# Two transformer layers in one kernel: where small loads, first tiles, projection banks and a norm's scale are placed

## The chip, the cores and the metric

The kernel runs on one core of a Trainium2 chip. The metric is the time of one execution on the device in microseconds (us); lower is better. A core has a matmul engine (TensorE; PE in the profile, PEld for its weight loads), VectorE (DVE), ScalarE (ACT), GpSimd (POOL) and SyncE (SP), which here only starts transfers. The engines run side by side, each through its own list of instructions in order, and wait for each other on semaphores.

## What is computed

Two batches of 1024 rows of 512 numbers, float32. Layer 1 is attention with 16 heads of 128 in a band of blocks, with a residual and a norm. Layer 2 picks 128 rows of each batch by a router's score and runs a full layer on those 256 rows only; the others pass unchanged, and everything is normed again. Since the second norm's input is x + x for a row that was not picked, and x is itself normed, its mean is nearly zero.

```python
x = layernorm(x + attention1(x, Wq, Wk, Wv, Wo))      # softmax over |block_i - block_j| <= 2, blocks of 64
scores = x @ w_router                                 # layer 2
idx = sort(top_k(scores, 128))                        # per batch
s = x[idx]
h = rms_norm(s, ln1_w)
q, k, v = h @ wq + bq, h @ wk + bk, h @ wv + bv       # rotated by position, causal over the 256 rows
x1 = s + attention2(q, k, v) @ wo
h2 = rms_norm(x1, ln2_w)
processed = x1 + silu(h2 @ w_gate) * (h2 @ w_up) @ w_down
gate = sigmoid(scores[idx])
out2 = x with rows idx set to gate * processed + (1 - gate) * s
x = layernorm(x + out2)
```

## The kernel before

**Numbers.** Matmuls of layer 1 and of the last stage work on pairs: ScalarE writes a rounded part ("hi", L1155), VectorE or GpSimd the rest ("lo", L1356 and L1664), and three products of the parts are summed (L885). Layer 2's projections and attention take plain float32 (L893).

**Order.** The program first writes one list of jobs, `order`, and every engine then walks the same list and emits its share. So the list fixes each engine's order, and a job placed early or late is so on all engines. `hold` and `freed` say who has to be done before a tile or a bank is written again. The main loop runs over u = 0 to END + 3 with END = 256: head H = u // 8 (0 to 31, two batches of 16), row tile i = u % 8. One step has three score matmuls, half a projection of q or k (`project_qk`), the transposes of the last tile's probabilities, the product with v, and, by its place in a group of two heads (16 steps), one tile of v (`project_v`) or of the output projection (`project_out`). On VectorE a step begins with the row maximum of the scores (L1391), and after ScalarE's exponential (L1193) come the scaling (L1400) and the lo parts. At the end of a step at most one piece of weights is split; two are when two are due.

**Start.** L724 to 739: eight tiles of x are loaded, four ahead of the first three weights and four behind; eight transposes (L912) into the eight banks, then the first projections of q and k, both into "proj0".

**Norms.** `finish_layer1` (L496) norms a tile of layer 1: statistics on VectorE (L1455, L1456), reciprocal root and shift on GpSimd (L1637, L1639, L1678), the row on ScalarE (L1239), the router's score on VectorE (L1465). `finish_plain` (L513) does the same for the second norm of rows that pass: job "pl", with four operations on GpSimd, and "plnorm" on ScalarE (L1246). For batch 0 this runs in steps 132 to 150, while batch 1's tiles are transposed in; for batch 1 the plain norms run in the last stage.

**Layer 2.** `choose` finds the rows and gathers them. `routed_in` has the gated rows' score and squares ("rin": L1522, L1525 on VectorE, an exponential on ScalarE L1261, L1637 and L1639 on GpSimd), the product with the norm's weights (L1533, followed by three small operations, L1537 to L1539) and four transposes (L1046), copied to hT ("rinh"). In step END - 4 = 252 stand, in this order: eight loads of layer 2's weights (`load_home`), the clearing of a tile for the biases (L1424), their load (L1772), that of the norm's weights (L1767), the split of the biases on ScalarE and VectorE, "rin" of batch 0; "rinh" follows in step 253. `project2` computes the projections of layer 2 in eight parts per batch, alternately in "proj0" and "proj1"; their bank is free when VectorE has rotated them (L1552 to L1556; v: when ScalarE has copied it). The rotated sum (L1557) is transposed (L1072). VectorE may rotate only when layer 1's last product with v is done, since the targets lie where layer 1's tiles are. The last stage is gate, up and down (`gate_up`, `down`).

## Time and profile before

| | us |
|---|---|
| median of 3 runs (1348.3 to 1349.73) | 1348.95 |
| the profiled execution | 1349.21 |
| its span, first to last instruction | 1347.5 |
| mean granted clock of the matmul engine | 0.985 |

| engine | share of the span | instructions |
|---|---|---|
| matmul engine | 95% | 7296 |
| VectorE | 59% | 2219 |
| ScalarE | 45% | 1422 |
| GpSimd | 18% | 234 |

The busy shares are means over stages that differ: in the steps of layer 1 the matmul engine has work all the time, in the change from layer 1 to layer 2 VectorE has. A time line row says when an instruction (or a run of equal ones, "x4") starts, how long it takes, the engine, the line of the kernel that emits it, and in brackets how long the engine had stood idle and who released it. Lines 885, 893, 1155, 1356 and 1664 are helpers, so a row is known by its tiles: "proj" is a projection bank, "s" scores, "o" products with v, "y" the output projection, "arena" the pairs, "wraw" raw weights, "late" layer 2's tiles, "works" working tiles. The clock is the granted one: 1.00 is 2.4 GHz, 0.50 is 1.2 GHz.

### The profile page before, as it was taken

Reading aid. Unit: us, or ns where it says so; the run is one execution under the profiler, and the core shown is the slowest. Engines: PE = TensorE matmul, PEld = TensorE weight load, DVE = VectorE, ACT = ScalarE, POOL = GpSimd, SP = SyncE. Lnnn points to the kernel's source line nnn. Section 1 sums busy time; section 2 is a strip of 40 time slices with the busy share of each in tenths; the row PEclk is TensorE's granted clock in tenths of the full one; section 3 lists DMA queues with packets and bytes.
Section 4 is the critical chain, followed back from the end, with each engine's and each line's share of the span. In section 5 each row is a group of like instructions: output and inputs, shape, how many; then the busy total and the mean of one; then the engine's idle time right before and its main releaser. Section 6 shows DMA issues by size and latency. Waiting matters only on the chain.

```text
span 1347.5 us, 19014 instructions
## 1 busy us (share of the span) xinstructions
PE 1280.1 (95%) x7296; PEld 1092.8 (81%) x7296; DVE 793.1 (59%) x2219; ACT 605.1 (45%) x1422; POOL 247.8 (18%) x234
## 2 busy tenths in 40 slices
PE   6999999999999999999999999999999858999897
PEld 5998989898989898977798989898989744445696
DVE  4656665666566656676767765666566557542244
ACT  4544445444444445445444444444544333434353
POOL 2111111111111101133121121111111121000186
PEclk9999999999999999999999999999999979999898
DMA  5110100110101202033210101010101225564064
GB/s 166 46 32 24 40 32 32 32 32 32 32 32 36 75 1 78 1 102 104 93 48 17 48 28 48 29 34 32 32 32 32 95 98 185 180 205 156 0 196 133
DMA packets 62411, 89.34 MB, mean 66 GB/s; under 512 B 3232, under 2 KB 36000, under 8 KB 62320
## 3 DMA queue, kind: packets, MB, share of 16 engines
q1 hardware_dynamic: 61904, 86.81, 19.8%
q0 software_dynamic: 416, 1.31, 0.3%
q8 instruction: 57, 0.93, 0.3%
q14 instruction: 34, 0.28, 0.1%
HBM read 79.20 MB, written 8.91 MB: 65 GB/s over the span
## 4 chain that ended last, share of the span: by engine, by line
PE 83%; DVE 8%; ACT 4%; POOL 2%; DMA 2%; issue 1%; SPq 0%; ACTq 0%; POOLq 0%; DVEq 0%
PE proj L885 38%; PE y L885 12%; PE o L885 9%; PE s L885 9%; PE tp L964 5%; PE proj L893 4%; PE s L893 3%; DVE arena L1356 2%; ACT arena L1155 2%; PE o L893 1%; POOL arena L1664 1%; DMA wraw<-in_L_ffn_w_up 1%; DVE prob L1391 1%; ACT prob L1193 1%; DVE products L1465 1%
## 5 line engine op out<-in xcount | busy, mean ns | idle before, releaser
L885 PE MATMUL proj<-arena 128*128 128x256 f32 (+1 forms) x3456 | 636.2, 333 | 6.8 <-DVE arena L1356 6.6
L885 PEld LDWEIGHTS proj<-arena 128*128 128x128 f32 x3456 | 529.2, 190 | 67.4 <-DVE arena L1356 10.6
L1193 ACT ACTIVATE prob<-prob,stat 128x384 f32<-128x384 f32 (+1 forms) x256 | 151.0, 590 | 445.0 <-DVE stat L1391 445.0
L1664 POOL TENSOR_TENSOR arena<-wraw,arena 128x1024 fp32r<-128x1024 f32 x75 | 181.8, 2432 | 841.3 <-ACT arena L1155 841.3
L1356 DVE TENSOR_TENSOR arena<-proj,arena 128x512 fp32r<-128x512 f32 (+1 forms) x262 | 146.5, 560 | 279.6 <-ACT arena L1155 278.2
L885 PE MATMUL y<-arena 128*128 128x512 f32 x762 | 198.6, 396 | 0.5 <-DVE yacc L1441 0.5
L885 PE MATMUL o<-arena 128*128 128x256 f32 (+2 forms) x960 | 196.4, 324 | 0.4 <-DVE arena L1356 0.2
L1356 DVE TENSOR_TENSOR arena<-tp,arena 128x384 fp32r<-128x384 f32 (+2 forms) x257 | 133.9, 521 | 103.9 <-ACT arena L1155 103.6
L885 PE MATMUL s<-arena 128*128 128x384 f32 (+2 forms) x870 | 191.1, 332 | 3.3 <-DVE arena L1356 3.2
L1155 ACT ACTIVATE arena<-proj 128x512 fp32r<-128x512 f32 (+1 forms) x262 | 127.6, 488 | 120.7 <-PE proj L885 114.8
L885 PEld LDWEIGHTS s<-arena 128*128 128x128 f32 x870 | 151.5, 188 | 20.8 <-DVE arena L1356 4.5
L885 PEld LDWEIGHTS y<-arena 128*128 128x128 f32 x762 | 138.6, 189 | 23.6 <-DVE yacc L1441 1.0
L885 PEld LDWEIGHTS o<-arena 128*128 128x128 f32 x960 | 136.8, 191 | 1.6 <-DVE arena L1356 1.1
L1391 DVE CUSTOM_DVE_ANT_0 prob<-s,band 128x384 f32<-128x384 f32 (+1 forms) x256 | 131.7, 515 | 0.7 <-PE s L885 0.7
L964 PE MATMUL tp<-ident,prob 128*128 128x128 f32 x704 | 119.8, 274 | 4.3 <-DVE prob L1400 4.3
L1155 ACT ACTIVATE arena<-tp 128x384 fp32r<-128x384 f32 (+2 forms) x257 | 117.4, 457 | 8.0 <-PE tp L964 7.9
L1400 DVE TENSOR_SCALAR prob<-prob,stat 128x384 f32<-128x384 f32 (+1 forms) x256 | 111.3, 435 | 9.1
L964 PEld LDWEIGHTS tp<-ident,prob 128*128 128x128 f32 x704 | 86.3, 140 | 21.1 <-DVE prob L1400 10.1
L1441 DVE TENSOR_TENSOR yacc<-y,yacc 128x512 f32<-128x512 f32 x127 | 87.1, 686 | 18.9 <-PE y L885 18.8
L1155 ACT ACTIVATE arena<-wraw 128x1024 fp32r<-128x1024 f32 x88 | 90.7, 1055 | 6.7 <-DMA wraw<-in_L_ffn_w_up 4.1
L893 PE MATMUL proj<-late 128*128 128x512 f32 x128 | 61.8, 606 | 4.0 <-DVE late L1556 4.0
L1155 ACT ACTIVATE arena<-o 128x512 fp32r<-128x512 f32 (+2 forms) x73 | 41.4, 567 | 27.1 <-PE o L1046 15.0
(153 smaller groups left out, 700.5 us busy)
## 6 DMA issues: line engine op xcount, KB each, us to landing
wraw<-in_L_attn_Wq SPq DMA_DIRECT2D x16, 512.0 KB, 3.4
wraw<-in_L_attn_Wk SPq DMA_DIRECT2D x16, 512.0 KB, 3.3
wraw<-in_L_attn_Wv SPq DMA_DIRECT2D x16, 512.0 KB, 3.3
wraw<-in_L_attn_Wo SPq DMA_DIRECT2D x16, 512.0 KB, 3.6
late<-in_L_ffn_wq SPq DMA_DIRECT2D x16, 512.0 KB, 4.7
late<-in_L_ffn_wo SPq DMA_DIRECT2D x16, 512.0 KB, 3.9
yacc<-in_L_attn_hidden_states SPq DMA_DIRECT2D x16, 256.0 KB, 3.0
y_dram<-yacc SPq DMA_DIRECT2D x16, 256.0 KB, 3.0
```

The costliest lines, as they stand in the source:

```text
L885: ins = e.matmul(out_ap, l[a], r[b], start=first and i == 0 and j == 0, stop=final and i == n - 1 and j == 2, skip_group_check=skip)
L893: ins = e.matmul(out_ap, l, r, start=first and i == 0, stop=final and i == n - 1, skip_group_check=skip)
L964: ins = e.transpose(bank["tp"][:, m * P:(m + 1) * P], prob[i % 2][:, m * P:(m + 1) * P], ident[:])
L1155: e.activation(dst, src, ACT.Copy).then_inc(*S_.inc(*name, "hi"))
L1193: e.activation(prob[s][:, 0:n], prob[s][:, 0:n], ACT.Exp, bias=stat[:, 4 * s + 1:4 * s + 2], scale=-1.0, accum_out=stat[:, 4 * s + 2:4 * s ...
L1356: e.tensor_tensor(dst_lo, src, dst_hi.bitcast(F32), ALU.subtract).then_inc(*V_.inc(*name, "lo"))
L1391: e.tensor_tensor_reduce(prob[s][:, 0:n], bank[f"s{s}"][:, 0:n], reach, -SCALE, -NEG, ALU.add, ALU.min, nm).then_inc(*V_.inc("scores", H, ...
L1400: e.tensor_scalar(prob[s][:, 0:n], prob[s][:, 0:n], rc, None, ALU.mult).then_inc(*V_.inc("norm", H, i, "prob"))
L1441: e.tensor_tensor(yacc[:, t, :], bank[bank_of["out", G, t]][:, :], yacc[:, t, :], ALU.add).then_inc(*V_.inc("out", G, t, "sum"))
L1465: e.tensor_tensor_reduce(products[:], row, router[:], 1.0, 0.0, ALU.mult, ALU.add, score[:, c:c + 1]).then_inc(*V_.inc("lnscore", b, t, "s ...
L1664: e.tensor_tensor(lo, wraw[n % RAW_SLOTS][:], hi.bitcast(F32), ALU.subtract).then_inc(*G_.inc("wsplit", n, "lo"))
```

## The change

- The biases' clearing and load (now job "ubraw") and the load of layer 2's first norm weights go from step 252 to step EARLY = 192. "rin" of batch 0 goes to step 250, its product ("rinx", split off from "rinh") to 251, the transposes and copy to 252, the biases' split to 253.
- At the start two weights are loaded behind x tiles 0 to 3, then tiles 4 to 7, then the third. Tiles 0 to 3 are transposed, then comes the first projection of q, tiles 4 and 5, that of k (in "proj1"), tiles 6 and 7.
- In the first group the projections of q go to bank "y", which the output projection doesn't use there; v's first part in layer 2, the third projection of batch 0, goes to "s1".
- The second norm's scale comes from the first's: with variance v and r = 1/sqrt(v + eps), the second scale on the normed row is 1/sqrt(v r r + eps/4). Three more operations on GpSimd in "ln" write it to eight columns of `stat`; job "pl" is gone; "plnorm" is a copy with that scale, without a shift.
- There are two tiles hT, one per batch.

The diff, cut (renamings and the same edit at further places are left out):

```diff
@@ placements of tiles
-        hT = whole(slot2, KT, P)
+        hT = [whole(slot2, KT, P), whole(slot0 + 2 * HD, KT, P)]
+        twice = stat[:, 8:8 + TT]
@@ project_qk: the bank is a parameter
-        def project_qk(H, which, c):
+        def project_qk(H, which, c, to="proj0"):
...
-            hold("proj0", ("qk", H, which, c), V_, "qk", H, which, c, "lo")
+            bank_of["qk", H, which, c] = to
+            hold(to, ("qk", H, which, c), V_, "qk", H, which, c, "lo")
@@ finish_layer1, finish_plain
+            hold(f"share{t % 2}", ("ln", b, t), G_, "ln", b, t, "twice")
             job("ln", b, t)
...
         def finish_plain(b, t):
-            hold(f"moments{t % 2}", ("pl", b, t), S_, "plnorm", b, t, "row")
-            job("pl", b, t)
             yield
@@ routed_in: jobs of batch 0 taken out, the product a job of its own
-            hold("work5", ("rin", b), T_, "rinh", b, "made")
-            hold("products", ("rin", b), V_, "rin", b, "score")
-            job("rin", b)
             if b == NB - 1:
+                hold("work5", ("rin", b), T_, "rinh", b, "made")
+                hold("products", ("rin", b), V_, "rin", b, "score")
+                job("rin", b)
                 for _ in range(RIN_STEPS):
                     yield "choose"
-            yield "choose"
+                yield "choose"
+            if b > 0:
+                job("rinx", b)
@@ project2
-            to = f"proj{n % 2}"
+            to = "s1" if (b, n) == (0, 2) else f"proj{n % 2}"
@@ start
         for t in range(4):
             load_resid(0, t)
-        load_next()
+        load_next(2)
         for t in range(4, TT):
             load_resid(0, t)
+        load_next()
         job("router")
-        for t, to in enumerate(("proj0", "proj1", "s0", "s1", "o0", "o1", "y", "tp")):
+        for t, to in enumerate(("tp", "s0", "s1", "o0")):
             turn_x(0, t, to)
-            if t == 3:
-                need("q", 0, 0)
-            if t == 5:
-                need("k", 0, 0)
+        need("q", 0, 0)
+        need("k", 0, 0)
         put(project_qk(0, "q", 0))
+        turn_x(0, 4, "o1")
+        turn_x(0, 5, "y")
+        put(project_qk(0, "k", 0, "proj1"))
+        turn_x(0, 6, "tp")
+        turn_x(0, 7, "o0")
         lo_engine[0] = lambda n: "G"
         need("v", 0, 0)
-        put(project_qk(0, "k", 0))
@@ steps: own is the bank of the q projections
+            own = "y" if G == 0 else "proj0"
...
-                    qk_gen = project_qk(H, "q", 1)
+                    qk_gen = project_qk(H, "q", 1, own)
...
-            if u == END - 4:
+            if u == EARLY:
                 hold("work1", ("ubias",), V_, "ubias", "lo")
                 bias_loaded.plan(0)
                 bias_loaded.plan(LO_ROW)
+                job("ubraw")
+                load_ln("work0", 0, V_, "rinx", NB - 1, "h")
+            if u == END - 6:
+                hold("work5", ("rin", 0), T_, "rinh", 0, "made")
+                hold("products", ("rin", 0), V_, "rin", 0, "score")
+                job("rin", 0)
+            if u == END - 5:
+                job("rinx", 0)
+            if u == END - 4:
+                put(routed_in(0))
+            if u == END - 3:
                 job("ubias")
-                load_ln("work0", 0, V_, "rinh", NB - 1, "h")
-                begin(routed_in(0))
@@ ScalarE: ubias, plnorm, rinh
-                    act.wait_ge(*V_.at("ubias", "zero"))
...
-                    act.wait_ge(*G_.at("pl", b, t, "shift"))
-                    e.activation(work[2 + i], yacc[:, t, :], ACT.Identity, bias=shift[i][:], scale=rstd[i][:]
+                    act.wait_ge(*S_.at("lnorm", b, t, "row"))
+                    act.wait_ge(*G_.at("ln", b, t, "twice"))
+                    e.activation(work[2 + i], yacc[:, t, :], ACT.Copy, scale=twice[:, t:t + 1]
...
-                    act.wait_ge(*T_.at("out", NB * NG - 2, TT - 1, "made"))
-                    if b > 0:
-                        act.wait_ge(*T_.at("p2", b - 1, len(QKV_ORDER) - 1, "made"))
+                    act.wait_ge(*T_.at("out", NB * NG - 2 + b, TT - 1, "made"))
@@ VectorE: ubraw is the clearing, ln alone takes statistics
+                elif kind == "ubraw":
+                    dve.wait_ge(*freed("work1", "ubias"))
+                    e.memset(work[1][0:BIAS_ROWS, :], 0.0).then_inc(*V_.inc("ubraw", "zero"))
...
-                elif kind in ("ln", "pl"):
+                elif kind == "ln":
@@ GpSimd: ln
+                    e.tensor_scalar(tmp[i][:], mv[i][:, 1:2], rstd[i][:], rstd[i][:], ALU.mult, ALU.mult
+                                    ).then_inc(*G_.inc("ln", b, t, "share"))
+                    pool.wait_ge(*G_.at("ln", b, t, "share"))
+                    e.tensor_scalar(tmp[i][:], tmp[i][:], 0.25 * LN_EPS, None, ALU.add).then_inc(*G_.inc("ln", b, t, "more"))
+                    pool.wait_ge(*G_.at("ln", b, t, "more"))
+                    if b > 0:
+                        pool.wait_ge(*S_.at("plnorm", b - 1, t, "row"))
+                    e.tensor_tensor(twice[:, t:t + 1], tmp[i][:], neg_half[:], ALU.pow).then_inc(*G_.inc("ln", b, t, "twice"))
@@ SyncE: the biases' loads hang on the new job
-                elif kind == "ubias":
-                    sp.wait_ge(*V_.at("ubias", "zero"))
+                elif kind == "ubraw":
+                    sp.wait_ge(*V_.at("ubraw", "zero"))
```

## Rows read from the trace of the kernel before

**Rows 1.** Page, part 1: busy time, share, instructions by engine.

```profile
PE 1280.1 (95%) x7296; PEld 1092.8 (81%) x7296; DVE 793.1 (59%) x2219; ACT 605.1 (45%) x1422; POOL 247.8 (18%) x234
```

**Rows 2.** Waits of the matmul engine: waiter <- releaser, us, times, longest.

```profile
PE proj L885 <- DVE arena L1356: 6.6, 9, 1.5
```

**Rows 3.** Stretches: length, busy time by engine, granted clock, DMA share, GB/s.

```profile
572.00:653.00 81.00, 73.38 (x408) 60.79 (x406) 58.61 (x160) 40.47 (x90) 28.37 (x58) 1.00 0.30 98
...
1089.70:1120.50 30.80, 28.75 (x115) 20.30 (x115) 19.21 (x62) 10.12 (x22) 8.45 (x19) 0.92 0.33 108
...
1275.00:1332.00 57.00, 57.00 (x413) 54.05 (x412) 27.90 (x35) 32.42 (x51) 43.29 (x46) 1.00 0.55 171
```

**Rows 4.** Time line, VectorE, 631.7 to 632.6: start, us, engine, instruction.

```profile
631.72 0.66 DVE L1455 BATCH_NORM_STATS2 bn_out<-yacc 128x6 f32<-128x512 f32 x1
...
632.51 0.39 DVE L1356 TENSOR_TENSOR arena<-proj,arena 128x256 fp32r<-128x256 f32 x1
```

**Rows 5.** Time line, all engines, 1066 to 1096.5 us.

```profile
1066.79 1.06 ACT L1155 ACTIVATE arena<-wraw 128x1024 fp32r<-128x1024 f32 x1
...
1068.05 0.68 DVE L1441 TENSOR_TENSOR yacc<-y,yacc 128x512 f32<-128x512 f32 x1
...
1069.01 0.60 ACT L1155 ACTIVATE arena<-proj 128x512 fp32r<-128x512 f32 x1 [1.16 <-PE proj L885]
...
1073.56 0.55 DVE L1391 CUSTOM_DVE_ANT_0 prob<-s,band 128x384 f32<-128x384 f32 x1
...
1076.60 0.48 DVE L1424 MEMSET works<- 40x512 f32 x1
...
1083.23 0.63 ACT L1155 ACTIVATE arena<-works 40x512 fp32r<-40x512 f32 x1 [7.83 <-DMA works<-bqkv]
...
1084.60 0.69 DVE L1522 CUSTOM_DVE_ANT_0 products<-x_sel,router 128x512 bf16<-128x512 f32 x1
...
1085.44 1.99 ACT L1155 ACTIVATE arena<-wraw 128x1024 fp32r<-128x1024 f32 x2
...
1086.83 5.11 POOL L1664 TENSOR_TENSOR arena<-wraw,arena 128x1024 fp32r<-128x1024 f32 x2
...
1086.88 2.84 DVE L1533 SCALAR_TENSOR_TENSOR works<-x_sel,gate,works 128x512 f32<-128x512 f32 x1 [0.49 <-POOL gate L1639]
...
1089.78 1.12 PE L1046 MATMUL proj<-ident,works 128*128 128x128 f32 x4 [15.08 <-DVE gate L1537]
...
1095.79 0.55 DVE L1391 CUSTOM_DVE_ANT_0 prob<-s,band 128x384 f32<-128x384 f32 x1
```

**Rows 6.** Instructions of line 1533, two executions: shortest, median, longest in ns.

```profile
L1533 DVE SCALAR_TENSOR_TENSOR works<-x_sel,gate,works x2: 731/1785/2839, 1086.9 to 1179.5; 128x512 f32<-128x512 f32 x2
```

**Rows 7.** Time line, all engines, the first 30 us.

```profile
9.86 1.22 DVE L1356 TENSOR_TENSOR arena<-wraw,arena 128x1024 fp32r<-128x1024 f32 x1 [0.26 <-ACT arena L1155]
...
12.21 1.97 PE L912 MATMUL o<-ident,yacc 128*128 128x128 f32 x8 [3.96 <-DMA yacc<-in_L_attn_hidden_states]
...
20.30 2.98 PE L885 MATMUL proj<-arena 128*128 128x512 f32 x12 [1.50 <-DVE arena L1356]
...
20.53 2.40 POOL L1664 TENSOR_TENSOR arena<-wraw,arena 128x1024 fp32r<-128x1024 f32 x1 [17.39 <-ACT arena L1155]
...
24.70 0.63 PE L885 MATMUL s<-arena 128*128 128x256 f32 x3 [1.41 <-DVE arena L1356]
...
27.95 0.69 PE L885 MATMUL s<-arena 128*128 128x384 f32 x3
```

**Rows 8.** Time lines of VectorE and the matmul engine, 1124 to 1130 us.

```profile
1124.63 0.69 DVE L1557 TENSOR_TENSOR late<-late 128x512 f32<-128x512 f32 x1
...
1126.74 0.69 DVE L1557 TENSOR_TENSOR late<-late 128x512 f32<-128x512 f32 x1
...
1124.65 3.07 PE L893 MATMUL proj<-late 128*128 128x512 f32 x4 [4.03 <-DVE late L1556]
...
1129.76 1.88 PE L893 MATMUL proj<-late 128*128 128x512 f32 x4
```

## What the change will do to the time

> **What bounds the kernel now.** I read the page first: the matmul engine is busy for 1280.1 of 1347.5 us [rows 1], so a gain can only come from the 67 us in which it stands still or runs slowly. The list of waits of that engine then gives the places: one wait of 15.08 us at the first transposes of layer 2, and nine waits on the low parts of layer 1 that sum to 6.6 [rows 2, 5]. The table of stretches shows a third sum: from 572 to 653 us, where batch 0 is normed and batch 1 is brought in, the engine works 73.38 of 81.00 us, 7.6 less than it could [rows 3]. The time lines of these places [rows 5, 7, 8] show what is late in each. In the last stage (1275 to 1332) the engine is busy 57.00 of 57.00 us [rows 3]: what is taken from other engines there is worth nothing. The profiled execution took 1349.21 us (span 1347.5 and 1.7 around it), the median is 1348.95; I work against 1349.2.
>
> **The small loads long ahead (steps 250 to 254): gain 10.2.** Now, in step 252, VectorE clears a tile, SyncE sends the biases behind eight weight loads, and ScalarE stands 7.83 us until they land; the gated rows' scores, squares and product stand behind that on VectorE, the transposes (L1046) behind them on the matmul engine [rows 5]. The change issues both loads 60 steps earlier (cost: a clearing of 0.48 us [rows 5], beside matmuls), and spreads the rest over steps 250 to 253. The 15.08 us don't all come back, because the steps from 251 on are short and run at VectorE's chain, not at the matmuls. I follow the row maximum of each tile on VectorE. Before, that of step 252 starts at 1073.56, that of 254 at 1095.79 [rows 5]. After:
> - Step 250 gets the gated rows' score and squares (2 x 0.69, [rows 5]) and ScalarE an exponential between them and its own work. The score can start when the sum at 1068.05 is over, 1068.7, and ends at 1069.4. Until then ScalarE may do neither the weight split that it now does at 1066.79 (1.06 us) nor the projection part that it now does at 1069.01 [rows 5]. So 1069.4 + 0.2 + 1.06 = 1070.7 for a part that ran at 1069.01: +1.7 on the chain.
> - Step 251 gets the product and three small operations. Alone the product takes 0.73, beside a split on GpSimd 2.84 [rows 6]. In this step GpSimd is likely through its one split; I take 0.73 and about 0.4 for the small ones: +1.1.
> - So the maximum of step 252 stands at 1073.56 + 2.8 = 1076.4. A tile takes 3.04 us on this chain (1073.56 to 1076.60, [rows 5]); two make 6.1. Into them go the first output sum (0.6), the bias parts (ScalarE 0.63, about as much on VectorE: 1.3), and two weight splits that now fill the standstill: 1.99 us on ScalarE, 5.11 on GpSimd [rows 5]. Of ScalarE's 1.99 I put 1.2 on the chain. That is 1076.4 + 6.1 + 0.6 + 1.3 + 1.2 = 1085.6 for 1095.79: 10.2.
> The gain holds the half clock too: the granted clock is 0.92 from 1089.7 to 1120.5 [rows 3], that is 5 of the 30.8 us at 1.2 GHz, behind the standstill. Bounds: without the +1.7 and 1.2, and with 0.5 less for the biases, 13.6; with VectorE held by the splits for 3.4 more, 6.8. The order on the matmul engine has the transposes one step earlier; its ready product comes before them, so they cost their own 0.65.
>
> First the row: the product starts at 1086.88, 0.05 us behind GpSimd's split, and takes 2.84 instead of 0.73 [rows 5, 6]. The Trainium skill (SBUF — State Buffer, section "SBUF: two separate sides") says that VectorE in a two-port mode or with two SBUF inputs and GpSimd lock a shared port for a whole instruction, and the other fully blocks. The trace agrees. By that rule the scalings of steps 253 and 254 could each be held for one split; it speaks against a full gain, and is the second rival below.
>
> **Start: gain 2.7.** Now the x tiles 4 to 7 come behind three weights, and the projections behind all eight transposes: tile 4 is turned at 12.21 and the first projection waits behind tile 7, although its weights' low part is ready at 9.86 + 1.22 = 11.08 [rows 7]. After: the query projection at 11.1 (its 12 matmuls take 2.98 by the second one's row, [rows 7]) to 14.1, two tiles of 0.85 each (half of 8 transposes in 1.97, less overlap) to 15.8, the key projection to 18.7 (in the second bank: no 1.50 us wait [rows 7]), two tiles to 20.4. First scores 24.70 to 20.4. But the value weights now land behind the x tiles and ScalarE splits them behind tile 7: about 22.2, so GpSimd's low part comes 22.3 to 24.7, where it now ends at 22.9 [rows 7]. The first value matmuls start at 24.8, the second scores at about 26.1 instead of 27.95: 1.85 stay. The third bank ("y", free in the first group) takes away two more waits of 0.4 each among the nine: 0.8. Sum 2.7; bounds 1.0 (value weights 1.7 later) and 5.1 (the whole 4.3).
>
> **One norm's scale from the other's (572 to 653): gain 4.5.** Per tile VectorE loses statistics and aggregate, 0.80 us from 631.72 to 632.51 [rows 4]; eight tiles make 6.4. ScalarE's plain norm stays in its place, but doesn't wait for GpSimd. The chain of this stretch lies mostly on VectorE and ScalarE; I take 0.56 of each 0.80, since ScalarE is next late: 4.5. Bounds: 1.0, where other waits take its place, and 7.6, where no standstill is left [rows 3]. GpSimd does three operations (some 1 us) more per norm and four fewer per plain norm; the additions stand behind the shift, so nothing of the same tile waits for them. Where two norms follow each other without a gap (tiles 6 and 7 of batch 1), the second shift comes 1 us later; its row of scores is needed over 10 us later. Batch 1's removed statistics lie in the saturated last stage: 0.
>
> **Third projection bank and two hT: gain 1.1.** The third projection of layer 2 starts at 1124.65 after a wait of 4.03 us for the rotation of the first, which frees its bank [rows 8]. In "s1" it runs in the wait, 1120.6 to 1122.2. The turning of the first needs VectorE's sum, which starts at 1124.63, that of the second the one at 1126.74 [rows 8]: the matmul engine reaches the third's second half at 1127.9 and not at 1129.76: 1.86. But it still stands most of 1122.2 to 1127.4, and its matmuls there run at half clock (3.07 us for four, [rows 8]); I keep 1.1, bounds 0.4 and 1.9. The second hT frees batch 1's copy from batch 0's last projection, which is long over by then: 0.
>
> **Sum.** 10.2 + 2.7 + 4.5 + 1.1 = 18.5: 1349.2 - 18.5 = 1330.7.
>
> **Rivals.**
> - The waits vanish more fully (0.17): ScalarE's part of the gate finds a gap, and VectorE had slack. 13.6 + 4.3 + 6.4 + 1.9 = 26.2: 1323.0. For it: the removed wait was of 15.08 and the clock came back late. Against: the 3.04 us pitch is already VectorE's.
> - GpSimd's splits block VectorE in the short steps, and ScalarE holds tiles and splits together (0.25): 6.8 + 2.0 + 3.0 + 0.4 = 12.2: 1337.0. For it: 2.84 against 0.73 [rows 6]. Against: the product slipped in between two splits.
> - It does not do what it says (0.07): the transposes stay late, because rows gathered, statistics and reciprocal root on GpSimd are behind a split, not the loads. Then only about 2 of the 10.2 come: 1338.9.
> - Slower (0.03): many standstills of 1 to 3 us from step 251 to 256 hold the clock at 1.2 GHz until about 1120. From 1089.7 to 1120.5 there are 28.75 us of matmul work [rows 3]; at half clock it takes as much again, 2.5 of which is paid now, and 2.3 for the 2.3 us of step 252 and 253 come on top. It decides from 21 us on: the whole gives 28.5 - 18.5 = 10 over, 1359. Against it: steps as thin as these ran within the stretch whose mean clock is 0.92 [rows 3].
> - The parts cancel to within 2.7 us (0.03): 1348.
> The forecast has 0.45, its own range 1326 to 1335. The range of 8 in 10 takes in most of the first two rivals: 1322 to 1339. A measurement can tell 0.2% (2.7 us) from no change: faster 0.94, same 0.03, slower 0.03.
>
> **What would show it.** The wait at L1046 for layer 2's first transposes under 2 us; the first scores near 20.4 and the second near 26.1; the maximum of step 254 about 10 us nearer to that of step 252; 572 to 653 shorter by 4.5; no wait above 3.5 us behind the last layer-1 output. Wrong if ScalarE stands behind the gate's exponential for more than 3 us, if the stretch of the norms keeps its length, or if a half clock appears between steps 250 and 256.

## The result

| | before | after |
|---|---|---|
| median (range), us | 1348.63 (1348.3 to 1349.73) | 1332.78 (1330.49 to 1335.49) |
| the profiled execution, us | 1349.21 | 1332.4 |
| its span, us | 1347.5 | 1330.3 |
| mean granted clock | 0.985 | 0.986 |

The ratio is 0.9882 (95% interval 0.9862 to 0.9902), 15.9 us; by the spans it is 17.2. The forecast was a gain of 18.5 us and a time of 1330.7. Part 1 of the page of after, which answers to [rows 1]:

```profile
PE 1279.7 (96%) x7296; PEld 1092.9 (82%) x7296; DVE 781.6 (59%) x2187; ACT 602.9 (45%) x1422; POOL 243.3 (18%) x218
```

The matmul engine has the same instructions and the same busy time to 0.4 us, so all of the gain is time in which it no longer stands. Its list of waits in after (waiter <- releaser, us, times, longest):

```profile
PE y L1097 <- DVE late L1582: 8.9, 6, 3.1
PE tp L989 <- DVE prob L1423: 7.1, 7, 1.9
PE proj L909 <- DVE arena L1379: 6.3, 8, 2.9
...
PE y L1097 <- ACT late L1184: 1.7, 1, 1.7
...
PE proj L1071 <- DVE gate L1562: 0.2, 1, 0.2
```

The wait of 15.08 us at layer 2's first transposes [rows 5] is 0.2 (last line). The low parts of layer 1 cost 6.3 where they cost 6.6 [rows 2], but 2.9 of them is one wait at the first projection, new by design. The longest entry is now layer 2's rotation, 8.9.

**Where the time went.** I took points that both traces have and subtracted their starts. A negative number in the last column is time that the stretch takes more than before.

| point | before | after | us sooner | added by this stretch |
|---|---|---|---|---|
| second scores of the start | 27.95 | 25.48 | 2.5 | 2.5 |
| weight split on GpSimd ahead of the norms | 536.08 | 533.06 | 3.0 | 0.5 |
| weight split behind the norms | 647.38 | 640.23 | 7.15 | 4.1 |
| row maximum of step 252 | 1073.56 | 1068.87 | 4.7 | -2.5 |
| row maximum of step 254 | 1095.79 | 1078.75 | 17.0 | 12.35 |
| last output products of layer 1 | 1118.89 | 1101.86 | 17.0 | 0.0 |
| first scores of layer 2 | 1134.03 | 1119.94 | 14.1 | -2.9 |
| last stage begins | 1267.39 | 1251.17 | 16.2 | 2.1 |
| end of the span | 1347.5 | 1330.3 | 17.2 | 1.0 |

*The start*, time line of the matmul engine in after (start, us, engine, instruction, idle before and its releaser), which answers to [rows 7]:

```profile
10.56 4.61 PE L909 MATMUL proj<-arena 128*128 128x512 f32 x12 [2.89 <-DVE arena L1379]
15.00 0.60 PE L936 MATMUL o<-ident,yacc 128*128 128x128 f32 x4
...
15.79 3.02 PE L909 MATMUL proj<-arena 128*128 128x512 f32 x12
...
20.32 0.59 PE L909 MATMUL s<-arena 128*128 128x256 f32 x3 [0.63 <-DVE arena L1379]
...
23.95 1.69 PE L909 MATMUL proj<-arena 128*128 128x256 f32 x12 [0.86 <-POOL arena L1690]
25.48 0.69 PE L909 MATMUL s<-arena 128*128 128x384 f32 x3
```

The first scores start at 20.32 (forecast 20.4), the second at 25.48 (26.1). But the first projection takes 4.61 us for the 12 matmuls that the second does in 3.02: the clock is half there, behind a standstill of 2.89. That the first scores still come where I put them is luck: the projection starts 0.5 us sooner than I counted, and tiles 4 and 5 take 0.4 us each (15.00 to 15.79) where I had 0.85, and so do tiles 6 and 7.

*The norms*, the stretch of after that answers to [rows 3] (length, busy time of PE, PEld, DVE, ACT, POOL, granted clock, DMA share, GB/s):

```profile
569.50:645.70 76.20, 71.85 (x406) 60.71 (x404) 53.23 (x143) 39.65 (x90) 27.88 (x52) 1.00 0.32 104
```

Nearly the same matmuls (406 for 408) lie in 76.20 us and not in 81.00; of the 7.6 us in which the engine stood, 4.35 are left (76.20 - 71.85). VectorE has 5.4 us less of work. The two windows don't begin and end at quite the same work; between the weight splits of the table, which do, the stretch is 4.1 us shorter.

*Steps 250 to 254*, time line of all engines in after, which answers to [rows 5], and one stretch of it:

```profile
1067.76 0.74 DVE L1558 SCALAR_TENSOR_TENSOR works<-x_sel,gate,works 128x512 f32<-128x512 f32 x1
...
1068.56 0.99 PE L1071 MATMUL proj<-ident,works 128*128 128x128 f32 x4 [0.19 <-DVE gate L1562]
...
1068.87 0.55 DVE L1414 CUSTOM_DVE_ANT_0 prob<-s,band 128x384 f32<-128x384 f32 x1
...
1071.08 2.01 ACT L1180 ACTIVATE arena<-wraw 128x1024 fp32r<-128x1024 f32 x2
...
1072.22 4.70 POOL L1690 TENSOR_TENSOR arena<-wraw,arena 128x1024 fp32r<-128x1024 f32 x2 [6.19 <-ACT arena L1180]
...
1074.57 0.15 DVE L1422 RECIPROCAL stat<-stat 128x1 f32<-128x1 f32 x1
1074.76 2.38 DVE L1423 TENSOR_SCALAR prob<-prob,stat 128x384 f32<-128x384 f32 x1
...
1078.75 0.56 DVE L1414 CUSTOM_DVE_ANT_0 prob<-s,band 128x384 f32<-128x384 f32 x1
```

```profile
1069.00:1075.00 6.00, 4.79 (x16) 3.98 (x15) 3.01 (x11) 5.27 (x12) 2.78 (x2) 0.50 1.00 377
```

The product takes 0.74 for 2.84 and the transposes run one step earlier. From the maximum of step 252 to that of step 254 it is 9.88 us, before it was 22.23. Two of the 9.88 are in one row: the scaling of step 253 takes 2.38 us while GpSimd splits; the usual length of this instruction is 0.42, as below.

The second fence shows that steps 252 and 253 run at half clock: 6.8 us of it, from 1068.7 to 1075.6. Before, there were 17.1 us of half clock at this place (1077.6 to 1094.7), most of it over the standstill. In after it costs nothing that can be seen: the matmul engine is busy for only 4.79 of these 6.00 us and waits for VectorE, and experiment 9 has the same 9.9 us from maximum to maximum with its half clock almost wholly behind them (1077.9 to 1081.4).

*Between the layers*, time line of the matmul engine in after, which answers to [rows 8], and two stretches of it:

```profile
1101.86 1.52 PE L909 MATMUL s<-arena 128*128 128x512 f32 x6
...
1103.43 1.88 PE L917 MATMUL s<-late 128*128 128x512 f32 x4
1108.45 0.63 PE L1097 MATMUL y<-ident,late 128*128 128x128 f32 x4 [3.14 <-DVE late L1582]
1110.76 1.11 PE L1097 MATMUL y<-ident,late 128*128 128x128 f32 x4 [1.69 <-ACT late L1184]
1111.67 3.62 PE L917 MATMUL s<-late 128*128 128x512 f32 x4
...
1115.94 3.78 PE L917 MATMUL proj<-late 128*128 128x512 f32 x4
...
1119.94 0.61 PE L917 MATMUL s<-late 128*128 128x128 f32 x4
```

```profile
1104.00:1109.00 5.00, 1.86 (x8) 0.66 (x6) 4.86 (x13) 0.83 (x2) 2.84 (x8) 1.00 0.80 277
1109.00:1120.00 11.00, 9.31 (x17) 4.09 (x17) 6.25 (x25) 2.49 (x4) 2.16 (x5) 0.53 0.25 85
```

The third projection's first half starts 1.57 us behind the last output products, without a wait, as planned; then the engine stands for 3.14 and 1.69 us, and from 1109.7 to 1120 (10.2 us) the granted clock is 0.5, 1.2 GHz, the half clock: four matmuls take 3.62 and 3.78 us instead of 1.88 and 1.98. Before, the same place had these rows (a stretch, and two of the time line):

```profile
1125.00:1129.00 4.00, 3.58 (x8) 1.42 (x6) 3.93 (x12) 1.20 (x2) 0.45 (x1) 0.57 0.08 11
```

```profile
1131.99 1.98 PE L893 MATMUL proj<-late 128*128 128x512 f32 x4
...
1134.03 0.61 PE L893 MATMUL s<-late 128*128 128x128 f32 x4
```

That is 3.4 us at half clock. From the last output products to the first scores ("the stretch between the layers" below) it was 15.14 us, it is 18.08: the part that I forecast at +1.1 stands at -2.9.

*The last stage.* It is 79.13 us long in after and 80.11 before. Its rows for the sum of the gated rows, before and then after, name the reason:

```profile
1337.54 0.75 DVE L1619 SCALAR_TENSOR_TENSOR works<-s,gate,works 128x512 f32<-128x512 f32 x1 [1.78 <-ACT works L1246]
```

```profile
1320.40 0.75 DVE L1645 SCALAR_TENSOR_TENSOR works<-s,gate,works 128x512 f32<-128x512 f32 x1 [3.21 <-PE s L909]
```

Before, the sum waits for the plain norm on ScalarE (L1246), which waits for GpSimd's shift; in after it waits for the last matmuls. The five profiles without the norm part all have the first wait (1.78 to 1.80) and a last stage of 79.9 to 80.3 us, the nine with it have the second and 78.4 to 79.2. So the norm part is worth another 0.8 to 1.9 us here. The 2.1 us ahead of the last stage are not the change's: 1.7 of them are a half clock at 1244.9 to 1248.3 in before, which eleven of the other twelve profiles have too, with or without the change, and this profile of after lacks.

### The profile page after: what moved, and what is told of

It reads as the page before. It is cut to its first block, busy times and chain, and to the rows that moved or that the text cites. A ratio compares the mean times of both kernels' runs of the same rounds, so it can differ in the third digit from the quotient of the medians.

```text
span 1330.3 us, 18968 instructions
## 1 busy us (share of the span) xinstructions
PE 1279.7 (96%) x7296; PEld 1092.9 (82%) x7296; DVE 781.6 (59%) x2187; ACT 602.9 (45%) x1422; POOL 243.3 (18%) x218
## 4 chain that ended last, share of the span: by engine, by line
PE 87%; DVE 7%; ACT 4%; issue 1%; POOL 1%; DMA 1%; SPq 0%; POOLq 0%
PE proj L909 41%; PE y L909 13%; PE s L909 10%; PE o L909 9%; PE tp L989 5%; PE proj L917 3%; PE s L917 3%; DVE arena L1379 2%; ACT arena L1180 2%; PE o L917 1%; ACT prob L1218 1%; DVE prob L1414 1%; DVE products L1490 1%; DVE prob L1423 1%; DVE yacc L1466 1%
## 5 line engine op out<-in xcount | busy, mean ns | idle before, releaser
L909 PE MATMUL proj<-arena 128*128 128x256 f32 (+1 forms) x3408 | 625.5, 332 | 7.2 <-DVE arena L1379 6.3
L909 PEld LDWEIGHTS proj<-arena 128*128 128x128 f32 x3408 | 521.8, 190 | 65.4 <-DVE arena L1379 8.2
L1379 DVE TENSOR_TENSOR arena<-proj,arena 128x512 fp32r<-128x512 f32 (+1 forms) x256 | 142.7, 558 | 274.2 <-ACT arena L1180 272.4
L909 PE MATMUL y<-arena 128*128 128x512 f32 x810 | 211.0, 396 | 0.3 <-DVE yacc L1466 0.3
L1180 ACT ACTIVATE arena<-proj 128x512 fp32r<-128x512 f32 (+1 forms) x256 | 124.3, 486 | 118.5 <-PE proj L909 115.5
L909 PEld LDWEIGHTS y<-arena 128*128 128x128 f32 x810 | 147.4, 189 | 24.7 <-DVE yacc L1466 0.7
L1466 DVE TENSOR_TENSOR yacc<-y,yacc 128x512 f32<-128x512 f32 x127 | 87.1, 686 | 17.1 <-PE y L909 17.0
L917 PE MATMUL proj<-late 128*128 128x512 f32 x120 | 58.6, 612 | 0.0
L1180 ACT ACTIVATE arena<-o 128x512 fp32r<-128x512 f32 (+1 forms) x74 | 42.0, 568 | 22.6 <-PE o L1071 14.7
```

The source lines that it names most:

```text
L909: ins = e.matmul(out_ap, l[a], r[b], start=first and i == 0 and j == 0, stop=final and i == n - 1 and j == 2, skip_group_check=skip)
L917: ins = e.matmul(out_ap, l, r, start=first and i == 0, stop=final and i == n - 1, skip_group_check=skip)
L1180: e.activation(dst, src, ACT.Copy).then_inc(*S_.inc(*name, "hi"))
L1379: e.tensor_tensor(dst_lo, src, dst_hi.bitcast(F32), ALU.subtract).then_inc(*V_.inc(*name, "lo"))
L1466: e.tensor_tensor(yacc[:, t, :], bank[bank_of["out", G, t]][:, :], yacc[:, t, :], ALU.add).then_inc(*V_.inc("out", G, t, "sum"))
```

## The experiments

Experiments 2, 7 and 8 start from the kernel before, the others from the changed kernel, and their edits are shown against the kernel that they start from (11 and 12 against the one ahead of them). All ratios are to the kernel before, run on the same chip.

**1. The changed kernel without its third bank.**

```diff
-            to = "s1" if (b, n) == (0, 2) else f"proj{n % 2}"
+            to = f"proj{n % 2}"
```

> The changed kernel with the third projection of layer 2 back in the first bank, all else as changed. Theory A, the third bank lengthens the half-clock time: in the changed kernel the matmul engine ran its one projection first and then stood twice (3.14 and 1.69 us) before 1111.7, and the granted clock was half from 1109.7 to 1120.0, where before it was half for 3.4 us. Then without the bank the standstill is one wait of 4 us again, the half clock short, and the median falls by about 3 us below 1332.8, to 1330. Theory B, the half clock there comes with the standstill of VectorE's rotation whatever the bank, and differs from run to run: the median is within 1.5 us of 1332.8 and the profile shows a half clock of some length behind the wait too; by the bank's own 1.1 us the median would be 1333.9.

Measured: 1331.31 us (1329.86 to 1334.51), ratio 0.986 [0.9844, 0.9877]; the whole change is at 0.9882 with an interval that overlaps. Its stretch between the layers is 17.79 us, with the wait that the kernel before had [rows 8] to 0.01 us:

```profile
1102.78 1.52 PE L909 MATMUL s<-arena 128*128 128x512 f32 x6
...
1108.56 3.78 PE L917 MATMUL proj<-late 128*128 128x512 f32 x4 [4.04 <-DVE late L1581]
```

With the same waits as before (4.04 and 0.69) the stretch is 2.65 longer than before. Its half clock is 10.2 us, before it was 3.4. So the long half clock can come without the bank. That the bank has no part in it isn't shown: this is one profile, and by the ratios (0.986 against 0.9882, intervals that overlap) the kernel is, if anything, 3 us faster without the bank. The table behind experiment 12 has all profiles.

**2. The bank alone, in the kernel before** (the same line, the other way round).

> The kernel before with the third projection of layer 2 in the bank s1 and nothing else. The stretch from the last output products to the first scores of layer 2 takes 15.1 us before, with 3.4 us at half clock in it. Theory A (the forecast): the third projection runs inside the wait, 1.1 us gained (0.4 to 1.9). Theory B, by the runs so far: the stretch is set by VectorE's second rotation and ScalarE's copy, and the bank moves matmuls only within it; 0 to 0.5 us at equal clock, and the median within 1 us of before, either way, by the length of the half clock.

Measured: 1350.62 us against 1350.17, ratio 1.0001 [0.9992, 1.001]: the bank is worth nothing, between -1.4 and +1.1 us. The time line of the matmul engine tells why:

```profile
1119.32 1.52 PE L885 MATMUL s<-arena 128*128 128x512 f32 x6
...
1120.89 1.88 PE L893 MATMUL s<-late 128*128 128x512 f32 x4
1125.90 1.08 PE L1072 MATMUL y<-ident,late 128*128 128x128 f32 x4 [3.12 <-DVE late L1557]
1128.01 1.09 PE L1072 MATMUL y<-ident,late 128*128 128x128 f32 x4 [1.03 <-DVE late L1557]
1128.89 3.62 PE L893 MATMUL s<-late 128*128 128x512 f32 x4
...
1135.00 0.61 PE L893 MATMUL s<-late 128*128 128x128 f32 x4
```

The third's second half starts 9.57 us behind the last output products; before it was 1129.76 - 1118.89 = 10.87. That is a gain of 1.3 us, where I counted 1.86 and kept 1.1. But these four matmuls take 3.62 us at half clock, which lasts 6.8 us here and 3.4 before, and the scores come 15.68 behind the products instead of 15.14.

**3. Does a shorter standstill keep the clock?** In the steps of the main loop `tick("p2r")` leaves the rotations out; in the last step (259) the first rotation is now advanced too, and so goes ahead of the last two output sums and their norms on VectorE.

```diff
-            tick("p2r")
+            tick(*(("p2r",) if u < END + 3 else ()))
```

> The changed kernel with the rotation of layer 2's first projection placed in the last step of the main loop (259), before the last two output sums and their norms on VectorE, and not after them. Theory A, the place in VectorE's order makes the 3.14 us wait and the half clock behind it: the rotation, ready some 10 us earlier, goes into VectorE's idle time near 1097 to 1102; the waits at the two transposes before 1111 fall under 1 us each, the half clock there is gone, and the median is 1332.8 - 4.8 (waits) - 3 (half clock) = 1325 to 1328. Theory B, VectorE has no slack there (it is the bound): what the rotation gains the last norms lose, the rows of scores come later, and the median stays within 1.5 us of 1332.8.

Measured: 1329.96 us (1329.54 to 1330.6), ratio 0.9856 [0.9839, 0.9872]. The stretch between the layers is 12.0 us, and its clock is whole (the stretch, then the time line):

```profile
1103.00:1116.00 13.00, 9.85 (x38) 5.40 (x37) 12.62 (x44) 4.50 (x7) 7.54 (x18) 1.00 0.63 198
```

```profile
1103.83 1.52 PE L909 MATMUL s<-arena 128*128 128x512 f32 x6
...
1106.20 0.66 PE L1097 MATMUL y<-ident,late 128*128 128x128 f32 x4 [0.63 <-DVE yacc L1466]
...
1111.09 0.63 PE L1097 MATMUL y<-ident,late 128*128 128x128 f32 x4 [2.51 <-DVE late L1582]
...
1115.83 0.61 PE L917 MATMUL s<-late 128*128 128x128 f32 x4
```

The first transposes wait for an output sum (0.63), which frees their bank, and no longer for the rotation (3.14). The 6.1 us that the stretch lost split into waits that went (3.14 + 1.69 - 0.63 - 2.51 = 1.7) and 4.4 that are nearly all the clock. This is one profiled execution; by the medians the gain is 2.8 and by the ratios 3.5, with intervals that just overlap, so in others the clock is likely low here or elsewhere (in this one the start had 6.8 us of it). The forecast of 1325 to 1328 was missed, and so was its sign that both waits fall under 1 us: the second is 2.51.

**4. The changed kernel once more**, beside the kernels of 8 to 10.

> The changed kernel itself, on the chip of the next three. By the runs so far its times spread from 1330.5 to 1335.5 where the kernel before spreads over 2 us. Theory: the spread is the length of the half clock in the thin stretches; this profile then shows the stretch from the last output products to the first scores of layer 2 between 16 and 18 us, by a half clock of 6.8 or 10.2 us, and a median of 1331 to 1335.

Measured: 1335.77 us (1332.7 to 1337.18), ratio 0.9884 [0.9869, 0.99]: the ratio holds (0.9882). The waits of the first and second transposes are 3.14 and 1.68, the stretch between the layers 18.09, the half clock 10.2 again.

**5. The norm part undone.** Statistics, job "pl" and the old "plnorm" are back.

```diff
-                elif kind == "ln":
+                elif kind in ("ln", "pl"):
...
-                    e.activation(work[2 + i], yacc[:, t, :], ACT.Copy, scale=twice[:, t:t + 1]
+                    e.activation(work[2 + i], yacc[:, t, :], ACT.Identity, bias=shift[i][:], scale=rstd[i][:]
```

> The changed kernel with the plain norm as before: its own statistics on VectorE and its own root on GpSimd, no scale from the first norm. Theory A, the removed statistics were on VectorE's chain where batch 0 is normed: the stretch between the two weight splits at 533 and 640 us is 4.1 us longer again and the median is 1332.8 + 4.1 = 1337. Theory B, the 4.1 us came from the third operand, the wait of ScalarE's plain norm for GpSimd, with the same sum. Theory C, the extra operations on GpSimd cost in the change between the layers (the second shift late by 1.3 us, ScalarE's copy behind it): then 4.1 - 1.3 = 2.8, 1335.6.

Measured: 1339.36 us (1337.51 to 1340.41), ratio 0.9926 [0.991, 0.9943]. From the weight split ahead of the norms (533.53) to the one behind them it is 111.33 us; in the kernel before 111.30, in after 107.17:

```profile
644.86 2.39 POOL L1689 TENSOR_TENSOR arena<-wraw,arena 128x1024 fp32r<-128x1024 f32 x1 [3.24 <-ACT arena L1181]
```

So the part is worth 4.2 us in its stretch. By the ratios it is 0.9926 - 0.9882 = 0.0044 or 5.9 us, and by the spans 5.5. More than the stretch is behind that: the wait for the plain norm at the end is back (1.79), and the last stage is 79.93 us long, 0.8 and 1.5 more than in the two profiles of the changed kernel.

**6. The bank "y" undone** (`own = "proj0"`).

> The changed kernel with all projections of q in the first group in the first bank again. Theory A (the forecast): bank y takes away two waits of 0.4 us, so the median is 1332.8 + 0.8 = 1333.6, and waits of projections on the low parts between 26 and 80 us are back. Theory B: nothing to measure, within 0.5 us, since the next wait takes their place.

Measured: 1333.89 us, ratio 0.9886 [0.9869, 0.9903], not to be told from the whole change. Between 24 and 80 us it has a wait of 0.42 at a projection and one of 0.28 at scores, where the changed kernel has one of 0.61 at scores. From the second scores to the same transposes near 81 us it is 56.05 us, in after 55.57: the bank is worth half a microsecond, less than a median shows.

**7. The new start alone** (with bank "y"), in the kernel before.

```diff
-        load_next()
+        load_next(2)
         for t in range(4, TT):
             load_resid(0, t)
+        load_next()
...
         put(project_qk(0, "q", 0))
+        turn_x(0, 4, "o1")
+        turn_x(0, 5, "y")
+        put(project_qk(0, "k", 0, "proj1"))
...
```

> The kernel before with the new start alone (two weights before tiles 4 to 7, projections between the transposes, q's projections of the first group in bank y). Theory A: 3.0 us, as the weight split at 536 us comes 3.0 sooner in the changed kernel; second scores at 25.5 instead of 27.95. Theory B: the start gains less where the clock is half over the first projection (3.4 to 6.8 us in four of the profiles): 1.5 to 3 by the run.

Measured: 1347.21 us against 1350.17, ratio 0.998 [0.997, 0.9989], that is 2.7 us (1.5 to 4.1). The weight split ahead of the norms comes at 533.33 instead of 536.08, 2.75 sooner. The first projection is slow here as well:

```profile
10.83 4.61 PE L890 MATMUL proj<-arena 128*128 128x512 f32 x12 [2.89 <-DVE arena L1362]
```

**8. The loads and the gated rows alone**, in the kernel before.

```diff
+            if u == EARLY:
...
+                job("ubraw")
+                load_ln("work0", 0, V_, "rinx", NB - 1, "h")
+            if u == END - 6:
...
+                job("rin", 0)
+            if u == END - 5:
+                job("rinx", 0)
...
```

> The kernel before with the small loads alone moved to step 192 and the gated rows' work to steps 250 to 253: no other part of the change. Theory A (the forecast): 9.8 to 10.2 us, 1348.6 - 10 = 1338.6, with the wait at the first transposes of layer 2 under 0.5 us, and the maximum of step 254 about 12.5 us behind that of step 252 instead of 22.2. Theory B, the part is worth its wait (15.1 and the half clock behind it): 1332. Theory C, it depends on the shorter norms before it: under 8.

Measured: 1340.39 us (1339.34 to 1341.97), ratio 0.9924 [0.9909, 0.994], 10.3 us. The maxima of the steps show both signs of the forecast:

```profile
1075.82 0.55 DVE L1405 CUSTOM_DVE_ANT_0 prob<-s,band 128x384 f32<-128x384 f32 x1
...
1085.71 0.56 DVE L1405 CUSTOM_DVE_ANT_0 prob<-s,band 128x384 f32<-128x384 f32 x1
```

Step 252 comes 2.3 us later than before, step 254 10.1 sooner (forecast: 2.8 later, and 1085.6 for 1085.71). The last output products start at 1108.91, 9.98 sooner; 0.28 of that is there at the weight split ahead of the norms (535.80 for 536.08), before the part begins, which leaves 9.7. The stretch between the layers is 15.34, with a half clock of 3.4 us.

**9. The gated rows long ahead.** "rin" and "rinx" of batch 0 in steps 216 and 217.

```diff
-            if u == END - 6:
+            if u == END - 40:
...
-            if u == END - 5:
+            if u == END - 39:
```

> The changed kernel with the gated rows' score, squares and product of batch 0 in steps 216 and 217 and no more in 250 and 251. Theory A (the sum of the prediction): in step 250 ScalarE stands for the exponential and does the weight split before the projection's part, and step 251 has the product; together they moved the row maximum of step 252 by 2.5 us. Early, these cost nothing beside the matmuls; the maximum of step 252 comes 2.5 us sooner and the median is 2 to 2.5 us below the changed kernel's. Theory B, GpSimd's splits block the scaling of step 253 wherever the rest stands (it took 2.38 for 0.42): then they take up part of it, and 0.5 to 1 us is left.

Measured: 1330.79 us, ratio 0.9848 [0.9833, 0.9863]. From the maximum of step 248 (1051.36) to that of step 252 (1068.20) it is 16.84 us, in the changed kernel on the same chip 19.33 (1050.75 to 1070.08): 2.49. This is the price of the gated rows in steps 250 and 251. It isn't all won: in their new place they cost 0.7, since from the weight split behind the norms to the maximum of step 248 it is 410.00 us here and 409.27 in the changed kernel (409.9 to 410.0 in all four profiles with the gated rows this early, 409.2 to 409.4 in the ten others). So the move nets 1.8. The medians differ by 5.0 (1335.77 to 1330.79) and the spans by 2.9; in the profiles 2.0 of that is a shorter half clock between the layers (6.8 us for 10.2). From step 252 to 254 it stays at 9.89, so the gated rows have no part in these.

**10. Both, 3 and 9.**

> The last one and the rotation of layer 2's first projection in step 259, together. Apart they gave 3.5 by the ratios (rotation) and, by the sum, 2.3. If they are independent the median is 1332.8 - 3.5 - 2.3 = 1327; if the rotation's gain is only the phase of the half clock, it is gone here in part: 1329 to 1330.

Measured: 1328.47 us (1327.69 to 1330.82), ratio 0.9832 [0.9818, 0.9845], between the two forecasts (1327; 1329 to 1330), and with an interval that overlaps that of experiment 9. The clock came back less well than in 3: the stretch between the layers is 15.11 and has a half clock of 6.8 us,

```profile
1110.00:1117.00 7.00, 7.00 (x11) 2.58 (x10) 3.90 (x20) 1.89 (x3) 2.43 (x5) 0.54 0.38 130
```

though the order of work there is that of experiment 3, with the same two waits (0.63 and 2.51), and there the half clock is missing.

**11. No weight splits in steps 252 to 254.** Added to 10; it tests whether GpSimd's splits hold VectorE.

```diff
-            else:
+            elif u < END - 4:
                 split_loaded(was_loaded)
```

> The kernel with both early parts, and without the two weight splits in steps 252 to 254 (they come behind the choice of rows). Theory A, they are what is left on the chain: in step 253 the scaling took 2.38 us for 0.42 beside GpSimd's split, and ScalarE's 2 us of splits held the exponential for 0.6; without them the maximum of step 254 comes 2.5 us sooner behind that of 252 (9.9 to 7.4) and the median falls from 1328.5 to 1326. Theory B, the output product's place on the matmul engine sets these steps: under 1 us.

Measured: 1324.68 us (1323.99 to 1326.69), ratio 0.9814 [0.9801, 0.9827]. VectorE in the kernel of 10, then in this one:

```profile
1073.43 2.39 DVE L1423 TENSOR_SCALAR prob<-prob,stat 128x384 f32<-128x384 f32 x1
```

```profile
1073.82 0.42 DVE L1423 TENSOR_SCALAR prob<-prob,stat 128x384 f32<-128x384 f32 x1
```

Without a split beside it the scaling takes 0.42 us, and steps 252 to 254 take 7.30 for 9.89: 1.97 from the scaling, the remaining 0.6 from the parts on ScalarE (two weights there take 2.01 us in one piece, behind which the exponential of step 253 comes 1.20 us behind its maximum and not 0.59). By the ratios the whole gain is 2.4 us.

**12. The best of these, with two more steps.** The value weights' low part at the start on VectorE, and the second rotation advanced ahead of the last stage.

```diff
-        lo_engine[0] = lambda n: "G"
         need("v", 0, 0)
+        lo_engine[0] = lambda n: "G"
...
+        tick(only="p2r")
         lo_engine[0] = lambda n: "V"
```

> The last one, with the second rotation of layer 2 placed before the last two norms on VectorE, and the low part of the first value weights on VectorE and not GpSimd. The second transposes of layer 2 lose their wait of 2.5 us, the first value products one of 0.9; sum against the last one 2.5 + 0.9 = 3.4 where no half clock stands in the stretch, so 1322.6. Rival: the rows of scores of tiles 6 and 7, 2.1 us later on VectorE, become the bound of the choice of rows: 1325.

Measured: 1325.05 us (1322.24 to 1325.34), ratio 0.981 [0.9797, 0.9823]. It is faster than the kernel before and the changed kernel, but isn't to be told from experiment 11; the forecast was 1322.6, and its rival gave 1325. The wait for the value weights (0.86) is gone, and the first two scores follow each other in 4.03 us instead of 5.18. The second transposes wait about as long as before (2.63 for 2.51), but they come sooner:

```profile
1103.05 0.63 PE L1098 MATMUL y<-ident,late 128*128 128x128 f32 x4 [2.63 <-DVE late L1583]
1103.51 5.30 PE L918 MATMUL s<-late 128*128 128x512 f32 x8
```

They start 5.66 us behind the last output products (1097.39), in experiment 11 it was 7.25. VectorE does take the second rotation 1.6 us sooner. But in experiment 11 the first half of the third projection (1.88 us) ran inside that wait; here it comes behind the transposes and makes a run of eight with the second half. So the first scores of layer 2 come 13.81 us behind the products, in experiment 11 13.56, and the gain is gone.

**All profiles, between the layers.** The time from the last output products to the first scores of layer 2, and the half clock in it:

| kernel | third bank | first rotation | half clock | stretch |
|---|---|---|---|---|
| before, 7, 8 | no | late | 3.4, 3.4, 3.4 | 15.14, 15.19, 15.34 |
| 1 | no | late | 10.2 | 17.79 |
| 2 | yes | late | 6.8 | 15.68 |
| 5, 6, 9 | yes | late | 6.8, 6.8, 6.8 | 15.94, 16.16, 16.12 |
| after, 4 | yes | late | 10.2, 10.2 | 18.08, 18.09 |
| 3, 10, 11, 12 | yes | early | 0, 6.8, 3.4, 3.4 | 12.00, 15.11, 13.56, 13.81 |

With the bank and the late rotation no profile has less than 6.8 us; without the bank three of four have 3.4. That speaks for a part of the bank in the long half clock, and experiment 1 against it; with one profile a kernel it stays open. The early rotation makes the stretch shorter in all four than it is in any with the bank and the late rotation.

## Why the prediction was right, and where it wasn't

The time came out 2.1 us above the forecast, within the forecast's own range; the gain was 15.9 us by the ratio, 2.6 short of 18.5. Two of the four terms have their measured size, that of the norm is right for its place and lacks another one, and the fourth isn't there. That the sum comes so close is in part luck, as the last part of this section says.

**Loads, forecast 10.2: right.** Alone they gave 9.7 us in the trace and 10.3 by the ratio; in the whole change 12.35 - 2.5 = 9.85. The inner steps hold too. Step 252 is late by 2.5 (forecast 2.8), and experiment 9 shows that it is the gated rows: 2.49. Steps 252 to 254 were put at 6.1 + 0.6 + 1.3 + 1.2 = 9.2; measured 9.88. The last term was sized by the wrong engine: I booked 1.2 us for two splits on ScalarE; experiment 11 gives 2.6 for all the splits, 1.97 of it as one blocked scaling on VectorE. That is the second rival's mechanism, seen once: two splits in a row on GpSimd take 4.70 us, and VectorE was held for most of the second. The scaling of step 254 took 0.42.

The other terms of the 9.2 were put at 8.0 together and are 7.30 in experiment 11, so two errors offset each other by half. The pitch of 3.04 us that I took for a tile is the distance from a maximum to a clearing, not to the next maximum; the maxima of steps 252 and 253 are 2.9 apart.

A scaling with one input in 32-bit numbers was held for 1.97 us, where the product that I cited has two inputs. The Trainium skill (SBUF — State Buffer, section "SBUF: two separate sides") names both kinds, an instruction in a two-port mode and one with two SBUF inputs, as holders of the shared port. By that rule the scaling is of the first kind; the trace agrees that it can be held (2.38 us for 0.42), and doesn't show its mode. The page says of GpSimd and VectorE alike that the one that is first blocks the other for the whole instruction; here the scaling started at 1074.76, near the start of the second split by an even division of the row (1072.22 + 4.70 / 2 = 1074.57), and ended at 1077.14, just behind that split's end at 1076.92. That fits; the row doesn't show where one split ends and the next begins.

**Start, forecast 2.7: right in sum.** Alone it gave 2.7 by the ratio and 2.75 in the trace. Errors inside it offset each other. The second scores are 2.5 sooner and not 1.85, because the value weights' low part was ready at 23.95 and not at 24.8. The query projection came at 10.56 and not 11.1, but took 4.61 us at half clock, where I took 2.98 from a row at full clock; the tiles behind it took 0.4 us each and not 0.85; and the bank "y" gave about 0.5 instead of 0.8.

**Norm, forecast 4.5: right in its stretch, and a term is missing.** 4.1 between the splits, and 4.2 when undone. The 0.56 of 0.80 us a tile was a choice; measured is 4.2 / 8 = 0.52. The step that failed is "Batch 1's removed statistics lie in the saturated last stage: 0". The stage is saturated only until the last matmuls; at its end VectorE stood 1.78 us for the last plain norm, and without that wait the stage is 0.8 to 1.9 us shorter over the profiles. Undone, the whole part costs 5.5 by the spans and 5.9 by the ratios.

**Third bank, forecast 1.1: wrong.** The step that failed is "the matmul engine reaches the third's second half at 1127.9 and not at 1129.76 ... I keep 1.1". Reaching it sooner is true: 9.81 us behind the last output products in after, 9.57 with the bank alone, 10.87 before. It was to be 1.86 and is 1.1 and 1.3. That it stays until the scores is false: from there to the first scores it was 4.27 before and is 8.27 in after (6.11 with the bank alone). I had read a half clock in the rows and treated it as a fixed property of the place, of a known length; its length is what changed, 3.4 before, 6.8 with the bank alone, 10.2 in both profiles of the changed kernel and in the one without the bank. Isolated, the bank gains 0.0 us (between -1.4 and +1.1). The -2.9 of the table of points is the clock's: the two waits sum to 4.83 us in after and 4.72 before, and the other 2.8 are matmuls that take longer. With the bank alone the waits are 0.57 shorter (4.15) and the matmuls 1.11 longer.

**The sum.** The parts by themselves give 10.3 + 2.7 + 5.5 + 0.0 = 18.5 us (the third by the spans of experiment 5), each known to 1 or 2 us, and the whole gives 15.9. What is lost on the way has the size of the 2.9 us between the layers, which none of the parts run alone has; that it is this loss isn't shown. The 17.2 of the spans is flattered: -2.9 between the layers stands there against +2.1 up to the last stage, of which 1.7 is a half clock that the profile of before has at 1244.9 to 1248.3 and that of after happens to lack. Against the forecast, an error of -4.0 between the layers is met there by 1.0 at the end of the last stage and by 2.1 that isn't the change's: that the spans come within 1.3 us of 18.5 is in part luck. The other runs of after reach from 1330.5 to 1337.2 where those of before mostly stay within 4 us: that fits half clocks of different length in one place, but I have a trace of only one execution of each series.

**Rivals.** "More fully" fell: ScalarE's part of the gate found no gap (2.5 lost). "GpSimd blocks" was true in kind, at 2.0 us where I had put 3.4. "Doesn't do what it says" fell with the wait at the transposes, 0.2. "Slower by half clock" put the half clock between steps 251 and 256. It was there, for 6.8 us over steps 252 and 253, and it was one of the prediction's signs of being wrong. But it cost nothing, since the matmul engine isn't the last there; the sign was badly chosen. The half clock that cost came behind the layer, 10.2 us at a price of about 4.4. Of the other signs, the first scores, the wait at the transposes and the waits behind the layer (3.31 at most) came out as said. "About 10 us nearer" for the maxima of steps 252 and 254 was 12.35; by the prediction's own working it should have read 13.0.

**What stays open.** Why the half clock lasts 3.4, 6.8 or 10.2 us. Experiments 3 and 10 have the same order of work in that place and the same waits, and one has none and the other 6.8. Whether the third bank makes it longer is open too, by the table behind experiment 12. No run here settles either.

## What to carry over

- A wait of 15 us on a bound engine is worth what the next chain leaves: follow the engine that will be last (here the row maximum on VectorE) step by step through the place. This gave 10.2 for a wait of 15.08, and 9.7 to 10.3 was measured.
- Work that is moved out of a full spot should go well beyond it. Six steps ahead the gated rows still cost 2.5 us, forty steps ahead 0.7; and the wait that was left was refilled by weight splits that cost 2.6.
- A stage that is saturated on average has an end where it is not. What is taken from the other engines is worth nothing up to the last matmul and can count behind it.
- Where the matmul engine is thin between two phases, count what you gain there at the end of the thin place, not inside it: the clock can take it back. Shortening the standstill itself (experiment 3, 3.5 by the ratios) gave more than keeping the engine busy around it (the bank, 0.0).

## What the runs showed of the hardware that I had not expected

- The granted clock falls to 0.5 also at the start, behind a standstill of 2.89 us that follows the transposes of the first four tiles: 12 matmuls in 4.61 us for 3.02. All eleven profiles with this start have them slow (4.44 to 5.49), but the column of the granted clock shows the half clock in five of them only and 1.00 in six: at this place the durations are the better witness.
- A half clock over steps 252 and 253 cost nothing: 9.88 us from maximum to maximum with 6.8 us of it, 9.89 in experiment 9 with its half clock almost wholly behind them.
- Between the layers the half clock lasted 3.4, 6.8 or 10.2 us, or was missing, with nearly the same order of work.
- A 128x384 scaling takes 0.42 us alone and 2.38 beside GpSimd's subtraction of two 128x1024 tiles, of which one takes 4.70 / 2 = 2.35: it waits out nearly a whole one.
